# Attention: the maxima turned one step later in a group, the weighted sums of two units back to back

## The reference

```
scores = einsum('bhqd,bhkd->bhqk', q, k) * scale
scores = where(causal, scores, -inf)
y_ar   = einsum('bhqk,bhkd->bhqd', softmax(scores, axis=-1), v)
```

## The kernel before, in words

| step | before: sums, turns and tiles | after: sums, turns and tiles |
|---|---|---|
| 0 | 9; tiles 10-12 | tiles 10, 11 |
| 1 | 10; 13-15 | 12 |
| 2 | 11; 16, 17 | 10+11; 13-16 |
| 3 | 18 | 17 |
| 4 | 0; turn of o1; 19-22 | turn of o1; 18, 19 |
| 5 | none | 0+1; 20-25 |
| 6 | 1; 23-26 | 26, 27 |
| 7 | 2; 27, 28 | 28 |
| 8 | 3; 29, 30 | 2+3; 29-32 |
| 9 | 31, 32 | 33, 34 |
| 10 | 4; turn of o0; 33-36 | turn of o0; 35 |
| 11 | 37 | 36, 37 |
| 12 | 5 | 4+5 |
| 13 | turn of the maxima; tile 0 | 0 |
| 14 | 6; 1, 2 | turn of the maxima |
| 15 | 3 | 1 |
| 16 | 7; 4, 5 | 6+7; 2-5 |
| 17 | 6 | none |
| 18 | 8; 7-9 | 6 |
| 19 | none | 8+9; 7-9 |

## Time and profile before

### The profile page before, as it was taken

How to read it: one execution, slowest core, us unless ns; L and a number is a source line. 1 busy time by engine, 2 the same in 40 slices (tenths; PEclk the granted TensorE clock), 3 DMA queues, 4 the chain that set the end, 5 groups by cost and what they waited for, 6 DMA issues and landing times. The chain is left out here.

```text
span 1883.9 us, 29315 instructions
## 1 busy us (share of the span) xinstructions
PE 1376.5 (73%) x8975; PEld 714.5 (38%) x8976; DVE 1286.4 (68%) x2984; ACT 833.7 (44%) x1181; POOL 866.1 (46%) x763
## 2 busy tenths in 40 slices
PE   4459999999999798683995857586666544592992
PEld 2113333333333576552894322132221101362991
DVE  4568898988884255673332179999999998671433
ACT  3405666666667211121453458457475232121551
POOL 3401111121211434375565237867868665573662
PEclk9658999999999688797997778798788766796996
DMA  4721111211141566442333286985867763723335
GB/s 129 243 80 51 43 62 38 61 45 52 51 71 37 81 93 96 134 105 87 83 91 93 60 227 152 244 198 150 223 151 193 190 153 78 181 92 110 92 91 150
DMA packets 219597, 214.96 MB, mean 114 GB/s; under 512 B 49504, under 2 KB 188739, under 8 KB 217155
## 3 DMA queue, kind: packets, MB, share of 16 engines
q1 hardware_dynamic: 197454, 184.90, 39.5%
q0 software_dynamic: 9216, 19.02, 3.2%
q10 hardware_dynamic: 12800, 9.46, 1.7%
HBM read 149.46 MB, written 63.37 MB: 113 GB/s over the span
## 5 line engine op out<-in xcount | busy, mean ns | idle before, releaser
L806 ACT ACTIVATE attn_prob<-attn_ps_cols 128x1024 f32<-128x1024 f32 (+1 forms) x320 | 290.5, 940 | 224.1 <-PE attn_ps_cols L682 222.7
L2340 POOL TENSOR_TENSOR ssm_hc<-ssm_h,ssm_cb 128x1024 f32<-128x1024 f32 x128 | 302.5, 2364 | 169.2 <-DVE ssm_h L2323 124.4
L2323 DVE TENSOR_TENSOR_SCAN ssm_h<-ssm_decay,ssm_ps_u 128x1024 f32<-128x1024 f32 x128 | 292.7, 2287 | 17.6 <-DVE ssm_ps_u L2318 0.5
L832 POOL TENSOR_SCALAR_AFFINE_SELECT attn_prob<-attn_prob 128x512 f32<-128x512 f32 x128 | 81.2, 634 | 421.4 <-ACT attn_prob L806 421.3
L714 DVE CUSTOM_DVE_ANT_0 attn_ps_rows<-attn_ps_rows,const_mask_rows 128x384 f32<-128x384 f32 (+3 forms) x512 | 235.5, 528 | 39.6 <-PE attn_ps_rows L649 39.6
L649 PE MATMUL attn_ps_rows<-attn_ks,attn_qs 72*128 72x512 bf16 (+3 forms) x768 | 225.7, 346 | 42.7 <-DMA attn_qs<-parts_dram 29.2
L2311 ACT ACTIVATE ssm_decay<-ssm_wide,ssm_aneg 128x1024 f32<-128x1024 f32 x128 | 146.0, 1146 | 181.5 <-DVE ssm_h L2323 121.0
L2274 PE MATMUL ssm_ps_u<-ssm_stack,ssm_spread 96*128 96x512 bf16 x256 | 96.2, 465 | 177.3 <-DVE ssm_h L2323 172.3
L682 PE MATMUL attn_ps_cols<-attn_qs,attn_ks 75*128 75x512 bf16 (+3 forms) x768 | 191.8, 330 | 4.8 <-DMA attn_qs<-attn_nrows 4.0
L701 PE MATMUL attn_ps_o<-attn_prob,attn_vw 128*32 128x512 f32 (+3 forms) x1536 | 164.3, 500 | 0.3 <-POOL attn_prob L832 0.3
L719 DVE TENSOR_REDUCE attn_nm<-attn_ps_rows 128x1 f32<-128x512 f32 x256 | 157.6, 684 | 5.8 <-PE attn_ps_rows L649 5.8
(11 more groups left out here) (331 smaller groups left out, 2473.1 us busy)
## 6 DMA issues: line engine op xcount, KB each, us to landing
ssm_wide<-delta_dram SPq DMA_DIRECT2D x128, 512.0 KB, 6.6
attn_ks<-parts_dram SPq DMA_DIRECT2D x48, 192.0 KB
attn_qs<-parts_dram SPq DMA_DIRECT2D x48, 192.0 KB
parts_dram<-proj_parts SPq DMA_DIRECT2D x8, 768.0 KB, 3.8
ffn1e_x<-ex_dram SPq DMA_DIRECT2D x40, 130.0 KB, 2.3
ffn2e_x<-ex_dram SPq DMA_DIRECT2D x40, 130.0 KB, 2.3
split_dram<-ssm_parts SPq DMA_DIRECT2D x6, 768.0 KB, 4.3
ssm_stack<-split_dram SPq DMA_DIRECT2D x18, 256.0 KB, 4.2
```

Of the source, the lines that this page charges most:

```text
L806: nc.scalar.activation(prob[u % RING][:, heads[0]:heads[-1] + 1, 0:w], ps_cols[s % 2][:].rearrange("p b (x q) -> p (b x) q", x=len(heads) ...
L2323: nc.vector.tensor_tensor_scan(h[t % H_RING][:], decay[t % DECAY_RING][:], ps_u[t % 2][:], 0.0, ALU.mult, ALU.add).then_inc(scan_done, 1)
L2340: nc.gpsimd.tensor_tensor(hc[:, t % HC_RING, :], h[t % H_RING][:], cb[b % 2][:], ALU.mult).then_inc(hc_done, 1)
```

## The change

`PV_LAG` gives way to a table `SUM_AT`, which names the step of each unit's weighted sum, always two units in one step. The turn of the maxima moves from step 13 to step 14, while the tiles of group g+2 still start at step 13 (`NEXT_STEP`). The row tiles are spread anew, since `slot_costs` follows the sums. The steps of `keep_o` and of the turns of o stay at 2 and 8, 4 and 10.

```diff
-PV_LAG = 3
+SUM_AT = {0: 5, 1: 5, 2: 8, 3: 8, 4: 12, 5: 12, 6: 16, 7: 16, 8: 19, 9: 19, 10: SPG + 2, 11: SPG + 2}
 EARLY = 10
 ROW_STEPS = 12
-TURN_STEP = 13
+TURN_STEP = 14
+NEXT_STEP = 13
...
-        pv_at[(ENDS[u] + PV_LAG) % SPG] = pv_at.get((ENDS[u] + PV_LAG) % SPG, 0) + 4 * rows_of(u)[1]
+        pv_at[SUM_AT[u] % SPG] = pv_at.get(SUM_AT[u] % SPG, 0) + 4 * rows_of(u)[1]
...
-ROWS_THERE = spread(list(range(EARLY)), range(TURN_STEP, SPG))
+ROWS_THERE = spread(list(range(EARLY)), range(NEXT_STEP, SPG))
 BANKS = 3
-KEEP_AT = (ENDS[UPG - 1] + PV_LAG - SPG, ENDS[3] + PV_LAG)
+KEEP_AT = (SUM_AT[UPG - 1] - SPG, SUM_AT[3])
...
-        late = [u for u in range(UPG) if ENDS[u] + PV_LAG >= SPG]
+        late = [u for u in range(UPG) if SUM_AT[u] >= SPG]
...
-                    if ENDS[u] + PV_LAG == s:
+                    if SUM_AT[u] == s:
                         weighted(g, k, u)
-                    if ENDS[u] + PV_LAG == s + SPG and g > 0:
+                    if SUM_AT[u] == s + SPG and g > 0:
                         weighted(g - 1, (k - 1) % STACKS, u)
```

## The result

The changed kernel took 2049.7 us (median of 4 runs) against 1985.2 us for the kernel before on the same chip: ratio 1.0271, 95% interval 1.0224 to 1.0318. A second set of runs, on another chip, gave 1951.9 against 1889.3 us: 1.0339, 1.0305 to 1.0373. Slower, as forecast, but by two to three times as much as the 22 us of the forecast.

The account below looks back on a forecast made before the run. TensorE was taken to bound part A, VectorE part B. Per group +1.80 and -0.25, 14 times, gave +21.7; with +0.5 at the end, +22 on the 1883.9 us span, plus 104.8 around it: 2011 us, range 1981 to 2021.

Parts of the forecast that it names:

- The walk: Start-by-start run through part A of a group period under the new order: 13.45 us against 11.65, taken as +1.80.
- The turn's wait: TensorE's wait before the turn of the maxima, behind VectorE's split; moving it one step later removes it: -1.06 us.
- The waits for ScalarE: In part A, columns of steps 15, 16 and 19 wait for exponentials: 0.53, 0.26, 0.45, together +1.24 us.
- Tile 10: Row tile in step 0 that needs tile 9's maxima finished; its wait grows to 0.80 us, +0.22.
- VectorE's idle place before tile 23: In part B, pair 0+1 in step 5 leaves VectorE about 0.85 us idle, against 1.14 before: -0.25 us.
- part B: Period from row tile 10 to the next tile 37, 18.43 us, VectorE-limited; claimed to change by -0.25 us.
- A join: Second weighted sum directly behind the first in a pair; saves 0.17 us, at least 0.16 and at most 0.21.
- the sum: Addition of part A +1.80 and part B -0.25 over 14 groups, +21.7, with +0.5 for the last two: +22 us.
- two signs named for a wrong forecast: Part A staying near 12.2 us, with no waits for ScalarE, or part B falling below 17.5 us.
- part A: Period from row tile 37 to tile 10, 11.65 us, TensorE-limited apart from two waits; claimed to grow by 1.80 us.
- where the sums land decides: Weighted sums of units 4 and 9 move from part B into part A, 5.82 us against 4.36: +1.46 us.
- what lies around the span: Time outside the profiled span, 104.8 us between 1883.9 and the runs' median 1988.7, untouched by the edit.

Follow-up runs that it names:

- filled kernel: Changed kernel with the first column half of steps 0, 1, 6, 7 and 8 multiplied two or three times into the same place; 1907.3 us, ratio 1.0117.
- filled kernel before: The kernel before the change with the same 7 repeated matmuls a group added, as a control; ratio 1.0015, not told from no change.

## Why the prediction was right or wrong

**Right: sign and mechanism of the order.** The walk gave parts of 13.45 and 18.2 us; at full clock they measured 13.29 and 18.02, a period of 31.31 against 31.6. Step by step:
- The turn's wait of 1.06 us went, as said. With the later turn alone 0.39 of it stayed, and the period fell by 0.67.
- The waits for ScalarE, absent in the earlier trace rows, came where the walk put them: 0.55, 0.25 and 0.46 us against 0.53, 0.26, 0.45 (the middle one from single starts: columns of step 16 at 341.42, PE free at 341.17).
- Tile 10: 0.80 against 0.80.
- VectorE's idle place before tile 23 came, 0.66 us against the 0.85 of the working (at 327.74 in VectorE's timeline), and it is the only one in part B, where 1.14 us stood before. This term was undersized: B fell by 0.41, not by 0.25.
- A join: 0.24 us saved, not 0.17, outside the upper bound of 0.21; a second sum follows with no gap to be seen. The Trainium skill's rule in "TensorEngine Tiling (Array Packing)", section "Key Properties", that a change of tiling mode drains the array, agrees with it: six changes fewer would save about 6 x 0.24 = 1.4 us of PE time, of which the longer waits leave nothing.

**Wrong: the size, by a term that wasn't there.** The step that failed is the sum: every term was priced at the 2.4 GHz level because the earlier trace rows had 1.00, no step asked whether the new order keeps it, and so falls of the clock stood at nothing without a reason. The clock fell for 10.3 us at a time, ten times between 180 and 650 us. That took 44.6 us, twice the whole forecast of 22. The filled kernel shows that it was this and not the places of the sums: same periods, no falls, 1.0117, against the +1.1% that the prediction had. The closeness of the last two is in part luck, for the interval is 1.0063 to 1.0172, and by the periods the order costs 14 x 1.24 = 17.4 us where the working had 21.7, 0.16 us a group too much in either part. Neither of the two signs named for a wrong forecast came (part A near 12.2, part B below 17.5), and no rival had this mechanism: a clock of 1.00 was taken as a fact and was a condition.

**Half right: "where the sums land decides".** Unit 9's move cost 0.79 us a group net with all that came with it, unit 4's nothing (29.37 against 29.40), since a join, what was left of the turn's wait and part B took it up. Bunching with no sum moved cost 1.20 (30.60 against 29.40), by the waits for ScalarE and at tile 10. So of the 1.91 us between the turn alone and the full-clock changed kernel, the moves explain less than half. The prediction had the sum of both right because it walked through the starts, and it named the smaller part as the cause. One sum alone taken out of part B shortened it by 0.46 or 0.50 us, both in the changed kernel by no more than 0.41; why two give back less than one isn't shown.

**Wrong, without effect on the sign: what lies around the span.** It is 2.1 us, not 104.8. The profile shown ahead and the timed runs came from chips at different levels, as the last section shows.

**Open.** That the falls carry the loss is shown; what brings one is not. It comes in some groups and not in their neighbours with the same order and the same busy time, and the kernel before has a stretch as idle in each steady group without one. Whether the missing weighted sum matters wasn't tried by itself, nor which of the five filled places is needed. Nor is it known what sets the two levels of the chips.

## What to carry to other kernels

Saving changes of array form is worth 0.24 us each here only if PE is the bound there and then; spread work that lets another engine catch up may be worth more where it is. When two engines share the bound, walk through the starts of one period, and keep a rival in which the clock doesn't hold, priced from rows at half clock: a clock of 1.00 in the old profile is no promise, and the busy time of a stretch didn't tell here which one brings a fall. A few repeated matmuls into the same place, in waits, are a cheap test of whether a loss is the clock's, if the old kernel with the same repeats stands beside it.

## What the runs showed of the hardware that was not expected

- The granted clock fell ten times between 180 and 650 us although no wait of PE there was longer than 0.8 us. The kernel before waits 1.06 us in front of each turn, and its clock stayed at 1.00. With repeated matmuls in five places of the period (PE busy 29.6 us of 31.3 in place of 28.4) it didn't fall.
- A fall lasts 10.3 us and makes a period of 31.3 us into one of 35.9.
- Chips have two levels for this kernel: 1888 and 1889 us, or 1985 and 1991. The attention periods are the same on both (the changed kernel at full clock: 31.31 us in its profiles of the first and of the second set). In the stages of the experts, the stretch from the first to the last transposition of the experts' inputs takes 112.0 us in the profile of before (897.3 to 1009.3) and 133.5 in that of the filled kernel before (924.4 to 1057.9), whose chip is at the 1991 level. It takes 134.0 in the changed kernel's first profile (1010.0 to 1144.0) and 112.9 in its second (958.9 to 1071.8). That is some 21 of the 100 us; where the rest lies wasn't taken apart.
